# Row maxima written straight into the stacked tile, reciprocals spread by four transfers, and a new order of work

## The reference

```
q = layernorm(x) @ Wq;  k = ctx @ Wk;  v = ctx @ Wv      # k, v repeated for 4 query heads each
x = x + softmax(q k^T / sqrt(32)) v @ Wo
h = bf16(layernorm(x));  qg, sg = quant(h * inv_gate);  qu, su = quant(h * inv_up)
g = (qg @ w_gate^T) * sg * s_wgate;  u = (qu @ w_up^T) * su * s_wup
i = bf16(clip(silu(g) * u, -10, 10));  qi, si = quant(i * inv_inter)
x = x + (qi @ w_down^T) * si * s_wdown
quant(y): scale = max(max|y| / 127, 1e-8) per token;  q = clip(round(y / scale), -127, 127)
```

## Time and profile before

| | |
|---|---|
| median of 3 runs | 769.38 us (763.32 to 770.7) |
| the profiled execution | 766.03 us, of which the span of its instructions 764.2 us |
| PE busy | 686.0 us, 90% of the span |
| DVE, ACT, POOL busy | 475.5, 285.9, 260.8 us |
| granted TensorE clock, mean | 0.969 |
| moved by DMA | 93.71 MB, 123 GB/s over the span |

### The profile page before, as it was taken

One profiled execution on the slowest core, in us unless ns is written; L12 is line 12 of the kernel. 1 busy time (PEld: TensorE's weight loads), 2 busy tenths in 40 slices (PEclk: granted clock), 3 DMA queues, 4 the chain that ended last, 5 costly groups with the idle time before them and its releaser, 6 DMA issues.

```text
span 764.2 us, 14196 instructions
## 1 busy us (share of the span) xinstructions
PE 686.0 (90%) x5840; PEld 449.4 (59%) x5840; DVE 475.5 (62%) x772; ACT 285.9 (37%) x449; POOL 260.8 (34%) x207
## 2 busy tenths in 40 slices
PE   3999999989899989999899979999899988997853
PEld 3989888867466646654556646664556543443321
DVE  4562514633566856786747665877647566967863
ACT  4443042373515242435133425253433334343221
POOL 3363130120315134334241534241543235355431
PEclk9999999999999999999989999999999989999967
DMA  9695633769442171235222363233312343211100
GB/s 344 207 364 169 215 98 109 222 216 298 118 167 57 36 223 34 81 94 166 63 80 69 80 177 80 50 101 119 101 47 80 122 118 79 97 57 62 53 27 27
DMA packets 45191, 93.71 MB, mean 123 GB/s; under 512 B 5176, under 2 KB 21560, under 8 KB 45112
## 3 DMA queue, kind: packets, MB, share of 16 engines
q1 hardware_dynamic: 42824, 84.43, 36.0%
q0 software_dynamic: 2304, 8.39, 2.8%
HBM read 70.65 MB, written 22.15 MB: 121 GB/s over the span
## 4 chain that ended last, share of the span: by engine, by line
PE 60%; DMA 21%; SPq 5%; DVE 4%; ACT 4%; POOL 3%; issue 2%; POOLq 0%; ACTq 0%
PE bank L788 14%; PE bank L701 14%; PE bank L814 6%; DMA wv_lo<-r_dram 5%; PE bank L663 4%; PE bank L676 4%; DMA k_stack<-k_dram 4%; DMA max_dram<-max_rows 3%; PE bank_s L720 3%; PE bank L836 3%; PE bank_o L752 3%; PE bank_s L738 3%; PE bank_d L757 3%; DMA r_dram<-r_sb 2%; PE bank L802 1%
## 5 line engine op out<-in xcount | busy, mean ns | idle before, releaser
L701 PE MATMUL bank<-act_t_hi,wq_hi 128*128 128x256 f16 x512 | 140.4, 274 | 0.0
L701 PE MATMUL bank<-act_t_lo,wq_hi 128*128 128x256 f16 x512 | 140.2, 274 | 0.0
L701 PE MATMUL bank<-act_t_hi,wq_lo 128*128 128x256 f16 x512 | 140.1, 274 | 0.0
L2191 DVE TENSOR_REDUCE neg_max<-bank_s 128x4 f16<-128x512 f32 x128 | 84.7, 684 | 54.2 <-PE bank_s L720 53.7
L1622 ACT ACTIVATE probs<-bank_s 128x512 f32<-128x512 f32 x128 | 73.0, 598 | 88.3 <-PE bank_s L738 66.7
L2808 POOL TENSOR_TENSOR wv_hi<-wv_hi,wv_lo 128x512 f32<-128x512 f32 x28 | 37.2, 1334 | 114.5 <-DMA wv_lo<-r_dram 108.2
L1658 ACT COPY q_t<-bank 128x1024 f16<-128x1024 f16 (+1 forms) x48 | 41.8, 871 | 74.3 <-PE bank L802 61.9
L2802 POOL TENSOR_TENSOR xs<-xb,inv_gate 128x1024 f32<-128x1024 bf16 x16 | 35.4, 2211 | 88.0 <-DVE xb L2221 88.0
L738 PE MATMUL bank_s<-q_stack,k_stack 97*128 97x512 f16 x128 | 45.1, 387 | 13.7 <-DMA q_stack<-max_dram 9.1
L701 PEld LDWEIGHTS bank<-act_t_hi,wq_hi 128*128 128x128 f16 x512 | 50.3, 98 | 10.3 <-issue 1.1
L701 PEld LDWEIGHTS bank<-act_t_lo,wq_hi 128*128 128x128 f16 x512 | 50.4, 98 | 9.6 <-issue 0.3
(11 more groups left out here) (145 smaller groups left out, 1372.1 us busy)
## 6 DMA issues: line engine op xcount, KB each, us to landing
q_stack<-q_dram SPq DMA_DIRECT2D x48, 256.0 KB, 4.4
inp<-in_x SPq DMA_DIRECT2D x16, 512.0 KB, 6.0
wv_lo<-r_dram SPq DMA_DIRECT2D x14, 512.0 KB
x<-in_x SPq DMA_DIRECT2D x11, 512.0 KB, 4.2
out<-x POOLq DMA_DIRECT2D x11, 512.0 KB, 3.0
q_dram<-q_st_hi SPq DMA_DIRECT2D x8, 512.0 KB, 4.0
q_dram<-q_st_lo SPq DMA_DIRECT2D x8, 512.0 KB, 5.1
w_gate<-in_ctx_t SPq DMA_DIRECT2D x6, 512.0 KB, 6.4
```

The costliest lines, as they stand in the source:

```text
L701: ins = nc.tensor.matmul(bank[:, :, jj, :], wq_sb[a][:, 2 * item + jj, kc, :], act_t[m][:, kc, :, :], start=(kc == 0 and (a, m) == PARTS[0 ...
L2191: nc.vector.tensor_reduce(neg_max[:, c:c + REP], bank_s[g % 2][:, :].rearrange("p (j n) -> p j n", j=REP), AX_X, ALU.max, negate=True).the ...
```

## The change

Three parts. The maxima go by one transfer from `max_rows` to row 96 of `q_stack`: 32 pieces of 128 numbers; `save_max` and `max_dram`'s semaphore are gone, and `mt_copy` waits for `max_stacked` instead. The reciprocals come back by four transfers of 32 partitions instead of one of 128. And the programs of all five engines are written in a new order. Besides, `pv(..., 0)` waits for `recip` of the batch before, where it waited for that of the batch before that.

```diff
-            return 32 * (r + 1) if is_first(p) else 16 * (r + 1) + 32
+            return 128 * (r + 1) if is_first(p) else 64 * (r + 1) + 128
...
-            def save_max(p, b):
-                r = 2 * p + b
-                sp.wait_ge(mt_out, r + 1)
-                sp.dma_start(max_dram, max_rows[:, :]).then_inc(max_saved, 16)
-
-            def fill_max(p, b):
-
-                r = 2 * p + b
-                sp.wait_ge(max_saved, 16 * (r + 1))
-                sp.dma_start(q_stack[SPLIT:SPLIT1, :, :, :].rearrange("p g t n -> p (g t n)"),
-                             max_dram.rearrange("h n -> (h n)").rearrange("(o n) -> o n", o=1)).then_inc(max_stacked, 16)
+            def fill_max(p, b):
+
+                r = 2 * p + b
+                sp.wait_ge(mt_out, r + 1)
+                sp.dma_start(q_stack[SPLIT:SPLIT1, :, :, :].rearrange("p g t n -> p (g t n)").rearrange("p (h n) -> p h n", n=P),
+                             max_rows[:, :]).then_inc(max_stacked, 16)
...
                 for t0, t1 in halves:
-                    rows = r_dram[r].rearrange("(g c) n -> g c n", g=4)[:, REP * t0:REP * t1, :]
-                    rows = rows.rearrange("g c n -> g (c n)").unsqueeze(1).broadcast_to([4, HD, (t1 - t0) * REP * P])
-                    sp.dma_start(r_rows(p, t0, t1), rows).then_inc(r_filled, 16)
+                    for g in range(4):
+                        rows = r_dram[r].rearrange("(g c) n -> g c n", g=4)[g, REP * t0:REP * t1, :]
+                        sp.dma_start(r_rows(p, t0, t1)[HD * g:HD * g + HD, :],
+                                     rows.rearrange("c n -> (c n)").partition_broadcast(HD)).then_inc(r_filled, 16)
...
-                if t == 0 and needed(r - 1):
-                    pe.wait_ge(recip_done, r - 1)
+                if t == 0 and needed(r):
+                    pe.wait_ge(recip_done, r)
...
-                    act.wait_ge(max_saved, 16 * r)
+                    act.wait_ge(max_stacked, 16 * r)
```

More of the change, by code:

```diff
@@ L473, in _ @@
-            fill_k(0, 1)
-            spill_k(6)
+            load_piece(7)
+            load_ctx(4, 0)
+            load_piece(9)
+            spill_v(1)
+            load_ctx(3, 1)
+            load_ctx(5, 1)
+            fill_k(0, 0)
+            load_ctx(5, 0)
+            load_piece(10)
+            load_ctx(6, 1)
+            load_piece(11)
+            spill_v(2)
+            fill_v(0, 0)
+            load_x(1, 1)
+            spill_k(2)
+            load_ctx(4, 1)
+            load_ctx(6, 0)
@@ L501, in _ @@
             load_piece(27)
-            fill_v(1, 0)
-            load_piece(28)
+            load_x(3, 1)
             load_piece(29)
             save_r(0, 1)
+            load_piece(28)
             load_piece(30)
-            load_res(1, 0)
[L508 to L513, removed]
+            fill_r(0, 1)
+            fill_v(1, 0)
+            load_piece(31)
+            fill_max(1, 0)
@@ L514, in _ @@
+            load_res(0, 0)
+            load_res(1, 0)
             load_x(4, 0)
+            load_res(0, 1)
+            fill_k(1, 1)
             fill_q(1, 1)
-            fill_k(1, 1)
+            save_r(1, 0)
+            load_x(4, 1)
+            fill_v(1, 1)
+            fill_r(1, 0)
             spill_q(2)
[L518 to L523, removed]
             fill_max(1, 1)
@@ L1026, in _ @@
-            q(3, 0, 2)
-            q(3, 0, 3)
-            wo_(0, 1, 1, 7, 8)
-            q(3, 1, 0)
+            q(3, 1, 3)
+            tq(0, 0, "g")
+            q(3, 2, 0)
             st(1, 1, 0)
             st(1, 1, 1)
-            q(3, 1, 1)
+            q(3, 2, 1)
             st(1, 1, 2)
+            q(3, 2, 2)
+            gu(0, 0, "gate")
+            q(3, 2, 3)
+            tq(0, 0, "u")
             st(1, 1, 3)
-            tq(0, 0, "g")
-            q(3, 1, 2)
+            q(3, 3, 0)
@@ L1037, in _ @@
+            q(3, 3, 1)
+            q(3, 3, 2)
             st(1, 1, 4)
+            gu(0, 0, "up")
+            q(3, 3, 3)
+            wo_(1, 0, 0, 0, 1)
+            st(1, 1, 5)
             pv(1, 1, 0)
-            st(1, 1, 5)
-            q(3, 1, 3)
+            wo_(1, 0, 0, 1, 3)
+            xt(4, 0, 0)
             st(1, 1, 6)
+            xt(4, 0, 1)
             st(1, 1, 7)
-            gu(0, 0, "gate")
-            tq(0, 0, "u")
-            q(3, 2, 0)
+            wo_(1, 0, 0, 3, 6)
@@ L1134, in _ @@
+            st(2, 1, 4)
+            pv(2, 1, 0)
+            gu(1, 0, "gate")
+            st(2, 1, 5)
+            tq(1, 0, "u")
+            xt(5, 1, 0)
+            xt(5, 1, 1)
             st(2, 1, 6)
             st(2, 1, 7)
-            q(4, 2, 1)
-            q(4, 2, 2)
-            dn(0, 1, 0)
-            dn(0, 1, 1)
+            gu(1, 0, "up")
+            wo_(2, 0, 0, 0, 3)
+            q(5, 0, 0)
+            wo_(2, 0, 0, 3, 4)
             pv(2, 1, 1)
+            wo_(2, 0, 0, 4, 5)
@@ L1275, in _ @@
-            xt(6, 1, 1)
+            st(4, 0, 5)
+            st(4, 0, 6)
+            q(6, 1, 1)
+            st(4, 0, 7)
+            q(6, 1, 2)
+            gu(2, 1, "up")
+            wo_(3, 1, 0, 0, 3)
+            q(6, 1, 3)
+            wo_(3, 1, 0, 3, 4)
+            pv(4, 0, 1)
+            wo_(3, 1, 0, 4, 5)
+            s(4, 1, 0)
+            wo_(3, 1, 0, 5, 6)
+            s(4, 1, 1)
+            wo_(3, 1, 0, 6, 8)
+            s(4, 1, 2)
+            wo_(3, 1, 1, 0, 2)
             s(4, 1, 3)
@@ L1358, in _ @@
+            st(5, 0, 7)
+            gu(3, 1, "gate")
+            q(7, 0, 0)
+            tq(3, 1, "u")
+            pv(5, 0, 1)
+            q(7, 0, 1)
+            gu(3, 1, "up")
             s(5, 1, 0)
+            wo_(4, 1, 0, 0, 2)
             s(5, 1, 1)
-            tq(3, 1, "g")
-            q(6, 3, 3)
-            xt(7, 0, 0)
+            wo_(4, 1, 0, 2, 3)
             s(5, 1, 2)
+            wo_(4, 1, 0, 3, 4)
             s(5, 1, 3)
-            gu(3, 1, "gate")
             s(5, 1, 4)
-            tq(3, 1, "u")
+            wo_(4, 1, 0, 4, 5)
@@ L2691, in _ @@
             quant(5, 0, 1)
+            ln2_stats(5, 1)
+            ln2_apply(5, 1)
+            gscale(5, 0, 0)
+            recip(6, 1)
+            quant(5, 1, 0)
             max_(7, 0, 0)
@@ L2885, in _ @@
             o_lo(1, 1, 0)
+            norm(1, 1, 1)
+            rstd1_(5, 0)
             fin(0, 0)
[L2887 to L2888 removed]
+            rstd1_(5, 1)
             rstd2_(1, 0)
@@ L2950, in _ @@
             rstd2_(4, 1)
+            norm(5, 0, 1)
             o_lo(5, 0, 1)
```

1865 lines of the change are left out of this document (898 added, 967 removed).

## The result

The changed kernel takes 739.11 us (median of 4 runs, 736.11 to 739.35); the kernel before, run beside it, 766.35 us. The ratio is 0.9635, with a 95% interval of 0.9565 to 0.9704: 3.7% faster. The forecast was 0.976.

What follows compares the result with a forecast made beforehand. PE was taken as the bound, busy 686.0 of 764.2 us, so only idle time and slow clock could be won. Terms -2 -6 -4.8 -5 -5.5 -2 +3 +4 = -18.3 us, scaled to 751 us; range 737 to 767.

Steps and rivals of the forecast that it cites:

- step (5): Start: context first lets `k(0, 0)` begin 3.8 us earlier, less up to 1.9 for eight transposes: 2 us won.
- step (2): Reciprocals' spread: lands in 4.5 us; values' wait of 4.8 us goes; some 2 of 4.4 us won before batch 15's projection.
- step (6): Tail: batch 14's up scaling and its chain come later behind `ln2_apply(7, 1)` and a quantization; 3 us charged.
- step (4): PE's slow clock behind the longer waits: 7.6 us of work lost, of which 5.5 us are taken back.
- Step (1): PE's waits for the maxima, 9.1 us: one transfer landing in 2.0 us takes back 6 and leaves 3.
- the four parts do not land earlier: Rival, chance 0.08: the new spreads land no sooner, so the waits for values and some maxima stay; 765 us.
- Step (3): Refill of stacked k and q: more work in the gap takes back 5 of 7.2 us of waits.
- Step (8): All engines: reordered steps that had room may lose it and cause new waits; 4 us charged (ends 0 and 15).
- more is won: Rival, chance 0.12: slack holds everywhere, no new waits, the tail costs nothing; 739 us.
- The signs for the maxima, the values, the refill, the tail and the mean clock: `q_stack` waits under 4 us, none for `v_cur`, `k_stack` 2; last `wo_` to end over 57; clock about 0.98.
- the share above 0.5: Sign: the DMA engines' busy share is above 0.5 while the four parts of the spread are in flight.

Runs made afterwards that it cites:

- the spread alone: Kernel before, in its old order, with the four transfers of 32 partitions for the reciprocals as the only change: 747.0 us, ratio 0.977.
- the kernel with the old tail: Changed kernel with the tail's order of before for VectorE, two steps of ScalarE and GpSimd: 734.2 us, ratio 0.962.

## Why the prediction was right, and where it was off

*The mechanism of the waits* was right: a transfer that uses few engines delays those behind it. Shown by the spread alone (17 us in the old order, my expectation was 10 to 16) and by the two transfers of 64 partitions. The sizes of the terms were mostly not right, and the sum came as near as it did because errors of both signs met. PE's idle time by stretch, from windows of both traces (us; the changes are taken before rounding):

| stretch | idle before | idle after | change | forecast |
|---|---|---|---|---|
| 0 to 40 us | 11.8 | 13.1 | +1.3 | -2, step (5) |
| 40 us to 13.8 us ahead of the last output projection | 36.2 | 14.4 | -21.7 | -6 -4.8 -5 +4 = -11.8 |
| the 13.8 us ahead of it | 5.6 | 4.6 | -1.0 | -2, step (2) |
| from it to the end | 24.6 | 27.7 | +3.0 | +3, step (6) |
| PE's busy time | 686.0 | 674.5 | -11.5 | -5.5, step (4) |
| all | | | -29.9 | -18.3 |

*Step (1), maxima:* 2.0 us taken for the landing, 1.8 measured. Of 9.1 us of waits I left 3 for crowded queues; 0.2 came. The crowd was mostly the wide spread itself, which I had counted as gone in one term and as present in the other: the spread alone took the waits to 0.8.

*Step (2), spread and the last projection:* the spread is no longer in the chain; `fin` and `rstd2` are, as predicted. The chain of the changed kernel ahead of the last projection:

```profile
664.23 0.76 DVE g_buf L2267
...
665.07 2.51 POOL x L2807 x2
...
668.50 0.57 POOL rstd L2772
669.07 2.46 POOL wv_hi L2793 x2
...
673.81 2.33 PE bank L767 x10
```

In idle time it gave 1.0 of the 2 us. One rival was summed up differently from the forecast: "the four parts do not land earlier" took away 4.5 us of the end, of which the forecast had counted only 2, so by its own terms it stood near 763 and not at 765.

*Step (3), refill:* 5 of 7.2 us taken back, 6.3 measured, less what hides in the 3.7 us without a name. That 2 us would remain for refills that meet a write of q was again too much. That 14 of 16 batches issued k behind q, and fewer do now, the prediction did not see.

*Step (4), clock:* 5.5 us taken; PE's busy time fell by 11.5. This is the largest miss. Between 250 and 675 us the granted clock is 1.00, where I had let a quarter of the 7.6 us stay, and I had left out the stretch after the wait for codes at 645 us. Windows of 10 us from 250 to 700 us of the kernel before give 8.9 us by the same product, so 2.6 of the 11.5 stay unexplained.

*Step (5), start:* this term was wrong in its sign. `k(0, 0)` was forecast near 10.0 and ran at 10.99, 2.8 us earlier than before; it waited for DVE's 2.09 us on the low weights, where I had put 1.2. But PE stood idle longer in the first 40 us, not shorter:

```profile
0.00:40.00 40.00, 28.17 (x235) 1.00 0.80 282
```
```profile
0.00:40.00 40.00, 26.88 (x227) 1.00 0.84 300
```

The first row is the kernel before, the second the changed one. Without the eight transposes ahead, the 11.0 us until `k(0, 0)` are all wait, and `xt(0, 1, 0)` waits 2.1 us more: 13.1 us, where 9.8 and 2.0 had been before.

*Step (6), tail:* +3 taken, +3.0 measured in idle time and +3.2 in length, 4.0 when it was undone.

*Step (8), new waits:* after the clock, the term that was farthest off. I charged 4 us. Of the 21.7 us in the middle stretch the three transfers' waits are 20.0; all other waits together fell by 1.7. New ones did come (3.7 us without a name, 1.2 for DVE, 1.0 for a split output), but older ones went, as those for ACT's probabilities (4.1 to 1.1 us).

So (1), (3), (4) and (8) were 15.9 us too cautious, and (2) and (5) 4.3 us too hopeful: 11.6 us in all, the difference between 18.3 and 29.9. The rival "more is won" named 739 us and was met by the number, partly by luck: its assumption on the tail did not hold, the start gave nothing, and the clock, which it let give 2 us more, gave 6. The signs for the maxima, the values, the refill, the tail and the mean clock (0.984) came as forecast; the share above 0.5 did not.

## What to carry to other kernels

Before anything is put in another order, look at the DMA share and the rate while one transfer is alone in flight. A share of a quarter at 72 GB/s said that a 512 KB transfer used about four engines, and splitting it, so that each part's outermost dimension is 32, was worth 17 us without any reordering. Splitting by itself is no gain: with two parts, whose outermost dimension is 2, the kernel was 12.5% slower. An order written by hand or by a planner carries the latencies it was made for: with the old transfers it was 2.4% slower, so transfers and order have to be changed, and judged, together. And when a part of an order is taken back in an experiment, every engine in that chain has to go back with it.

## What the hardware did that I had not expected

The new order with the wide spread was 33 us slower than with the narrow ones, far more than the 9.4 us of waits for the maxima behind it. A late transfer that GpSimd waits for also holds the engines that wait for GpSimd: ScalarE's waits for `norm` grew from 25.6 to 46.6 us (`wk_hi`) and from 10.7 to 21.6 (`o_t_hi`). How much of the 33 us passes this way is not measured.

One VectorE instruction of the tail, which takes 0.81 us elsewhere, took 4.85 us while GpSimd ran its four instructions of 669.0 to 673.8 us (and 4.85 or 4.86 us in three other kernels with this tail and the four transfers):

```profile
669.45 4.85 DVE L2206 TENSOR_SCALAR xb<-kv_st,mv,rstd 128x1024 bf16<-128x1024 f32 x1
```
```profile
669.04 2.49 POOL L2793 TENSOR_TENSOR wv_hi<-wv_hi,wv_lo 128x512 f32<-128x512 f32 x2
671.50 2.25 POOL L2798 TENSOR_TENSOR wk_lo<-wv_hi,wk_hi 128x512 f16<-128x512 f32 x2
```

It ended 0.5 us after them. In the kernel with the old tail the same instruction started only near the end of GpSimd's four, took 1.40 us, and again ended 0.5 us after them:

```profile
671.83 2.26 POOL L2798 TENSOR_TENSOR wk_lo<-wv_hi,wk_hi 128x512 f16<-128x512 f32 x2
```
```profile
673.23 1.40 DVE L2206 TENSOR_SCALAR xb<-kv_st,mv,rstd 128x1024 bf16<-128x1024 f32 x1
```

By the Trainium skill ("SBUF — State Buffer", SBUF: two separate sides) VectorE in its faster modes of two ports and GpSimd share a pair of ports: whichever instruction starts first holds it to its end, and the other is blocked. Both pairs of rows fit that only if VectorE's instruction did not get the ports between GpSimd's, which stand without a gap. No run keeps VectorE's instruction and takes GpSimd's away, so that one holds up the other is what the rows suggest, not shown.
